# D times u as a diagonal TensorE product that opens the state-sum bank, in a fused attention, Mamba and FFN kernel

## The reference, cut to what matters

```python
def step(h, inp):
    dt_t, B_t, C_t, u_t = inp
    dA = jnp.exp(dt_t[..., None] * A)
    h = dA * h + (dt_t * u_t)[..., None] * B_t[:, None, :]
    y_t = jnp.einsum('ben,bn->be', h, C_t)
    return (h, y_t)
...
y = ys.transpose(1, 0, 2) + u2 * D_param
y = y * jax.nn.silu(z)
out = jnp.einsum('ble,ed->bld', y, W_out)
```

## Time and profile before

| | |
|---|---|
| median of 3 runs | 778.05 us (777.77 to 780.21) |
| the profiled execution's own time | 779.12 us |
| its span (first to last instruction) | 777.3 us |
| mean granted TensorE clock | 0.989 |
| busy: TensorE, VectorE, ScalarE, GpSimd | 713.9, 685.4, 640.2, 608.8 us |

### The profile page before, as it was taken

The page is one execution under the profiler, slowest core; times in us unless marked ns, Lnnn a source line. Parts: engine busy times, 40 slices in busy tenths (PEclk is TensorE's granted clock), DMA queues, the critical chain, the costliest instruction groups (busy, mean ns, idle before and its releaser), DMA issues. The chain is left out here.

```text
span 777.3 us, 21855 instructions
## 1 busy us (share of the span) xinstructions
PE 713.9 (92%) x8036; PEld 406.7 (52%) x8036; DVE 685.4 (88%) x1138; ACT 640.2 (82%) x1282; POOL 608.8 (78%) x598
## 2 busy tenths in 40 slices
PE   6889999998999989999999999979998999887888
PEld 4676644644565446556555356445464453352456
DVE  6987428998999999899999899999999999898983
ACT  4778687999989999998889999888979866865633
POOL 5004336888998989778898789999999999999871
PEclk9999997999999999999999999999999999999999
DMA  6000014442624152323415161525261525344410
GB/s 212 3 4 2 3 45 151 132 128 87 186 68 156 36 175 95 100 95 110 138 47 192 52 229 58 178 89 175 68 192 45 177 83 177 109 153 136 149 42 28
DMA packets 45003, 83.63 MB, mean 108 GB/s; under 512 B 5081, under 2 KB 5730, under 8 KB 44898
## 3 DMA queue, kind: packets, MB, share of 16 engines
q1 hardware_dynamic: 44898, 82.25, 33.1%
HBM read 71.22 MB, written 11.01 MB: 106 GB/s over the span
## 5 line engine op out<-in xcount | busy, mean ns | idle before, releaser
L1804 POOL TENSOR_TENSOR d<-d,cr 128x1024 f32<-128x1024 f32 x128 | 299.9, 2352 | 16.1 <-DVE d L1305 5.8
L1622 ACT ACTIVATE ps<-dt,An 128x512 f32<-128x512 f32 x252 | 172.2, 696 | 39.6 <-DVE d L1305 38.5
L1305 DVE TENSOR_TENSOR_SCAN d<-ps,hl,d 128x512 f32<-128x512 f32 x128 | 157.6, 1267 | 3.7 <-ACT ps L1622 3.2
L1305 DVE TENSOR_TENSOR_SCAN d<-ps,d 128x512 f32<-128x512 f32 x128 | 150.1, 1207 | 6.6 <-ACT ps L1622 6.2
L886 PE MATMUL ps<-h,w 128*128 128x512 f16 (+1 forms) x512 | 114.5, 376 | 8.5 <-DVE h L1237 8.2
L1293 DVE TENSOR_TENSOR d<-ps,du 128x512 f32<-128x512 f32 x173 | 112.2, 675 | 6.1 <-PE ps L975 3.8
L1790 POOL TENSOR_TENSOR d<-du,br 128x512 f32<-128x512 f32 x79 | 99.8, 1274 | 8.3 <-PE ps L975 5.4
L886 PEld LDWEIGHTS ps<-h,w 128*128 128x128 f16 x512 | 47.7, 98 | 77.8 <-DVE h L1237 20.8
L975 PE MATMUL ps<-d,cst 128*32 128x512 f32 x512 | 68.1, 604 | 2.9 <-POOL d L1804 2.9
L897 PEld LDWEIGHTS ps<-w,h 128*128 128x128 f32 x496 | 58.2, 192 | 8.3 <-issue 5.5
L824 PE MATMUL ps<-cst,sx 128*128 128x128 f32 x384 | 56.1, 283 | 6.1 <-ACT sx L1453 4.1
(11 more groups left out here) (185 smaller groups left out, 1374.7 us busy)
## 6 DMA issues: line engine op xcount, KB each, us to landing
cr<-bcd SPq DMA_DIRECT2D x64, 256.0 KB, 3.3
br<-bcd SPq DMA_DIRECT2D x64, 256.0 KB, 3.2
dt<-dtd SPq DMA_DIRECT2D x64, 256.0 KB, 3.6
du<-dud SPq DMA_DIRECT2D x64, 256.0 KB, 3.7
dtd<-sR SPq DMA_DIRECT2D x16, 256.0 KB, 2.6
dud<-sE SPq DMA_DIRECT2D x16, 256.0 KB, 2.0
X<-in_x SPq DMA_DIRECT2D x8, 256.0 KB, 6.1
out<-X SPq DMA_DIRECT2D x3, 512.0 KB, 4.6
```

Of the source, the lines that this page charges most:

```text
L1305: eng.tensor_tensor_scan(d, banks[u % NG][:, :], d, hl[:, r:r + 1] if m % 2 else 0.0, ALU.mult, ALU.add).then_inc(v_sc, 1)
L1622: eng.activation(banks[u % NG][:, :], src[:, :], ACT.Exp, scale=An[:, g:g + 1]).then_inc(s_da, 1)
L1804: eng.tensor_tensor(d, d, CR[k % NC][:, :].unsqueeze(1).to_broadcast((128, n, 512)), ALU.mult).then_inc(p_cm, n)
```

## The change

`csum_t` at w = 0 (blocks 0 to 14) first multiplies u by a 128 x 128 diagonal matrix of D_e on TensorE, into the whole bank with `start=True`; the sixteen sums of a block then add to it. VectorE's step (`gate_v`, in `yev_v`'s places) multiplies the bank by silu(z) straight into u's buffer, now waiting for `s_zs` too. GpSimd's `gate_p` goes, and all that waited for `p_gt` waits for `v_yg`. GpSimd builds the diagonals once (`dd_p`). To make room the constant `spread` goes; GpSimd builds a wider 128 x 512 form of it (`spr_p`) in the tenth D buffer before the scans begin, and the products of `bdt_t` and `bdu_t` use all 128 rows. No other place of the table changes.

```diff
-    (BLOCKS[:-1], 'gate_p yev_v'),
+    (BLOCKS[:-1], 'gate_v'),
...
+    "dd_p": [33000],
+    "spr_p": [105500],
...
+            fours = D[:, ND - 1, :]
             def bdt_t(u):
+                if u > 1:
+                    eng.wait_ge(v_dr, u - 1)
                 bank = bank_of["bdt", u] = turn((s_da, u + 1))
                 eng.wait_ge(v_md, 2)
-                q = slice(32 * u, 32 * u + 32)
-                eng.matmul(bank[:, :], spread[q, :], sR[q, :], start=True, stop=True).then_inc(t_bdt, 1)
+                if u == 0:
+                    eng.wait_ge(p_spr, 1)
+                eng.matmul(bank[:, :], fours[:, 128 * u:128 * u + 128], sR[:, :], start=True, stop=True).then_inc(t_bdt, 1)
...
                 bank = bank_of["y", m, eb]
+                whole = (m, eb) != BLOCKS[-1]
+                if w == 0 and whole:
+                    if k == 0:
+                        eng.wait_ge(p_dd, 2)
+                    eng.wait_ge(s_silu, m + 1)
+                    eng.matmul(bank[:, :], Dd[:, eb, :], u2[m % 2][:, eb, :], start=True, stop=False, skip_group_check=True)
...
                     t = eng.matmul(bank[32 * q:32 * q + 32, :], csel, D[:, (4 * k + q) % ND, :],
-                                   start=(w == 0), stop=(w == 3))
+                                   start=(w == 0 and not whole), stop=(w == 3), skip_group_check=True)
...
-                eng.wait_ge(p_gt, 2 * m + 2)
+                eng.wait_ge(v_yg, 2 * m + 2)
...
+                if u == ND - 1:
+                    eng.wait_ge(t_bdt, FIRST)
+                    eng.wait_ge(t_bdu, FIRST)
...
-            def yev_v(m, eb):
-                if m == eb == 0:
-                    eng.wait_ge(l_w2, 16)
-                yg = u2[m % 2]
+            def gate_v(m, eb):
+                eng.wait_ge(s_zs, m + 1)
                 eng.wait_ge(t_y, 8 * m + 4 * eb + 4)
-                eng.scalar_tensor_tensor(yg[:, eb, :], yg[:, eb, :], Dp[:, eb:eb + 1], bank_of["y", m, eb][:, :],
-                                         ALU.mult, ALU.add).then_inc(v_yg, 1)
+                eng.tensor_tensor(u2[m % 2][:, eb, :], bank_of["y", m, eb][:, :], zs[m % 2][:, eb, :], ALU.mult).then_inc(v_yg, 1)
...
+            def spr_p():
+                eng.wait_ge(v_set, V_END)
+                eng.wait_ge(l_w1, 16)
+                eng.tensor_scalar(D[:, ND - 1, :].rearrange("p (c s) -> p c s", s=4), ident.unsqueeze(2).to_broadcast((128, 128, 4)), 1.0, 0.0, ALU.mult, ALU.add).then_inc(p_spr, 1)
...
-            def gate_p(m, eb):
-                yg = u2[m % 2]
-                eng.wait_ge(s_zs, m + 1)
-                eng.wait_ge(v_yg, 2 * m + eb + 1)
-                eng.tensor_tensor(yg[:, eb, :], yg[:, eb, :], zs[m % 2][:, eb, :], ALU.mult).then_inc(p_gt, 1)
+            def dd_p():
+                eng.wait_ge(l_w1, 16)
+                eng.wait_ge(l_w2, 16)
+                for eb in range(2):
+                    eng.tensor_scalar(Dd[:, eb, :], ident, Dp[:, eb:eb + 1], None, ALU.mult).then_inc(p_dd, 1)
```

More of the change, by code:

```diff
@@ L23 @@
 CONST, NCONST = {}, 0
-for _name, _n in (("ident", 128), ("qmask", 4), ("csel", 32), ("one8", 1), ("rmask", 2), ("spread", 128)):
+for _name, _n in (("ident", 128), ("qmask", 4), ("csel", 32), ("one8", 1), ("rmask", 2)):
     CONST[_name] = (NCONST, _n)
@@ L167 @@
     ([(0, g) for g in range(8)], 'aqm_v'),
-    ([()], 'an_s lpre_p one_v vz_p'),
+    ([()], 'an_s dd_p lpre_p one_v spr_p vz_p'),
     (BATCH_HALVES[2:], 'aln_v'),
     ([(u,) for u in range(NCORE) if driver(u) == "v"], 'drive_v'),
-    (BLOCKS[:-1], 'gate_p yev_v'),
+    (BLOCKS[:-1], 'gate_v'),
     ([(NCORE - 1,)], 'out_v'),
@@ L382 @@
     "lmo_t": [730212, 731403],
+    "gate_v": [170724, 203947, 243372, 289687, 329072, 373421, 412775, 455280, 491228, 541367, 573401, 605514, 645916, 678023, 713280],
+    "dd_p": [33000],
     "lpre_p": [719305],
@@ L472, in const @@
             return cst[0:rows, at:at + n]
-        ident, qmask, csel, one8, rmask, spread = (const(n) for n in ("ident", "qmask", "csel", "one8", "rmask", "spread"))
+        ident, qmask, csel, one8, rmask = (const(n) for n in ("ident", "qmask", "csel", "one8", "rmask"))
         masks = sb("masks", [128, 288], BF16)
@@ L558, in hybrid_block @@
         hl = sb("hl", [128, NR])
+        Dd = sb("dd", [128, 2, 128])
         l_x = [sem(f"l_x{i}") for i in range(2 * NB)]
@@ L566, in hybrid_block @@
         l_t, l_q = ([sem(f"l_{x}{q}") for q in range(4)] for x in "tq")
-        v_set, v_clr, v_one, p_set, p_vz, s_ap = (sem(n) for n in ("v_set", "v_clr", "v_one", "p_set", "p_vz", "s_ap"))
+        v_set, v_clr, v_one, p_set, p_vz, s_ap, p_spr = (sem(n) for n in ("v_set", "v_clr", "v_one", "p_set", "p_vz", "s_ap", "p_spr"))
         v_ast, v_aag, p_ars, s_ano, p_ano, t_atr, s_aat, p_aap = (sem(n) for n in ("v_ast", "v_aag", "p_ars", "s_ano", "p_ano", "t_atr", "s_aat", "p_aap"))
@@ L580, in hybrid_block @@
         t_mx, s_mx, t_md, s_md, v_md, p_md, s_bp = (sem(n) for n in ("t_mx", "s_mx", "t_md", "s_md", "v_md", "p_md", "s_bp"))
-        s_da, v_dr, p_dr, v_sc, p_hl, p_cm, t_y, v_cm, v_yg, p_gt, p_lp, v_lg, t_mo, v_mo, t_bdt, t_bdu = (
-            sem(n) for n in ("s_da", "v_dr", "p_dr", "v_sc", "p_hl", "p_cm", "t_y", "v_cm", "v_yg", "p_gt", "p_lp", "v_lg", "t_mo", "v_mo", "t_bdt", "t_bdu"))
+        s_da, v_dr, p_dr, v_sc, p_hl, p_cm, t_y, v_cm, v_yg, p_dd, p_lp, v_lg, t_mo, v_mo, t_bdt, t_bdu = (
+            sem(n) for n in ("s_da", "v_dr", "p_dr", "v_sc", "p_hl", "p_cm", "t_y", "v_cm", "v_yg", "p_dd", "p_lp", "v_lg", "t_mo", "v_mo", "t_bdt", "t_bdu"))
         V_SEL, V_FFN, V_WK, V_END = 7, 17, 20, 20
@@ L958, in bdu_t @@
                 eng.wait_ge(p_md, 3)
-                q = slice(32 * u, 32 * u + 32)
-                eng.matmul(bank[:, :], spread[q, :], sE[q, :], start=True, stop=True).then_inc(t_bdu, 1)
+                if u == 0:
+                    eng.wait_ge(p_spr, 1)
+                eng.matmul(bank[:, :], fours[:, 128 * u:128 * u + 128], sE[:, :], start=True, stop=True).then_inc(t_bdu, 1)
             def csum_t(k):
@@ L999, in lmo_t @@
                 bank = bank_of["lmo", h] = banks[0 if h else 3]
-                eng.wait_ge(p_gt, 2 * NM - 1)
+                eng.wait_ge(v_yg, 2 * NM - 1)
                 eng.wait_ge(p_lp, 2)
@@ L1347, in _ @@
                     "fln_v": fln_v, "flo_v": flo_v, "fl1_v": fl1_v, "fl3_v": fl3_v, "mln_v": mln_v, "dt_v": dt_v, "dr_v": dr_v,
-                    "drive_v": drive_v, "scan_v": scan_v, "yev_v": yev_v, "mout_v": mout_v}
+                    "drive_v": drive_v, "scan_v": scan_v, "gate_v": gate_v, "mout_v": mout_v}
             for name, at in plan:
@@ L1554, in mz_s @@
                 if m >= 2:
-                    eng.wait_ge(p_gt, 2 * m - 2)
+                    eng.wait_ge(v_yg, 2 * m - 2)
                 for eb in range(2):
@@ L1824, in _ @@
             mine = {"vz_p": vz_p, "lpre_p": lpre_p, "aln_p": aln_p, "aap_p": aap_p, "akp_p": akp_p, "jsub_p": jsub_p, "jsum_p": jsum_p, "jmix_p": jmix_p, "fln_p": fln_p,
-                    "mln_p": mln_p, "dt_p": dt_p, "du_p": du_p, "drive_p": drive_p, "out_p": out_p, "gate_p": gate_p}
+                    "mln_p": mln_p, "dt_p": dt_p, "spr_p": spr_p, "du_p": du_p, "drive_p": drive_p, "out_p": out_p, "dd_p": dd_p}
             for name, at in plan:
```

3 lines of the change are left out of this document (removed).

## The result

| | before | after |
|---|---|---|
| median | 778.2 us (4 runs, 777.77 to 780.21) | 785.66 us (4 runs, 782.93 to 787.16) |
| profiled execution, span | 779.1, 777.3 us | 787.16, 785.3 us |
| mean granted clock | 0.989 | 0.989 |

The ratio of after to before is 1.0067, 95% interval [1.0036, 1.0097]; the two medians by themselves are 0.96% apart, at the upper end of that interval, as four runs of each are few. The forecast was 778.0 us, between 772 and 784.

The account below looks back on a forecast made before the run. No engine bounds the whole: TensorE and ScalarE carry 240 to 480 us, VectorE bounds 480 to 717. Terms -0.5 - 0.7 + 2.5 + 0.5 - 1.5 - 0.3 = 0.0 us gave a median of 778.0 us, between 772 and 784 8 times in 10.

Parts of the forecast that it names:

- the term of the diagonal product: TensorE, fifteen block openings: 14.7 us more work, priced at 2.5 us for five openings and 0.5 us for ten.
- For the other ten ... taken as 0.5 us: Ten openings outside 240 to 480 us: 0.5 us lost, bounds 0 to 9.8, with 23.6 us TensorE free in 480 to 717.
- the openings from 240 to 480: Five openings where TensorE has 7.9 us free: 2.5 us lost, the middle of bounds 0 and 4.9.
- GpSimd's gate: 15 GpSimd instructions, 19.2 us, removed: 0.5 us won through VectorE's waits for GpSimd, bounds 0 and 4.2.
- The turn at the drive near 706: GpSimd's drive at 706.37 would wait for sums until 707.0, so the pairs behind it come 0.6 us later than now.
- VectorE's step: Fifteen block ends on VectorE, 682 instead of 726 ns each: 0.7 us won, bounds 0 and 0.7.
- The product's length: Each diagonal product on TensorE takes 0.98 us, read from a similar identity product in the trace.
- The first tiles: Before the first scans, 128-row products longer but clock kept up (6 in 10): 1.5 us won, bounds 2.9 won, 2.1 lost.
- Constants and load: Building constants on GpSimd costs nothing, `spr_p` at most 1.28 us in a 9.11 us gap; smaller load wins 0.3 us.
- The first, with 784: Five openings in 240 to 480 cost 4.9 us, first tiles lose 2.1: 784 us; 0.32 including its halves.
- The second (773): GpSimd's relief from 480 to 717 frees VectorE of 4.2 us, clock gives 2.9: 773 us; faster side 0.32.
- The signs that the forecast named for being wrong: VectorE's idle time from 142 to 740 us changing by more than 3 us, or the clock falling at new places.

Follow-up runs that it names:

- e4: Changed kernel with the diagonal product moved behind the first four sums of its block; 1.0076 [1.0053, 1.01] to the kernel before.
- e7: Changed kernel with GpSimd kept busy by a same-size product at each old gate's place; 1.0052 [1.0031, 1.0073] to the kernel before.
- e8: Changed kernel with 79 instead of 126 filler products between 609 and 715 us; 1.0055 [1.0035, 1.0076] to the kernel before.
- e2: Changed kernel without its fifteen diagonal products, u D left out; 0.9957 [0.9932, 0.9982] to the kernel before.
- e12: Changed kernel without diagonal products, GpSimd kept busy at its old gate's places, first run; 0.999 [0.9973, 1.0008] to the kernel before.
- e13: Changed kernel without its diagonal products, run again on another chip; 0.9961 [0.9939, 0.9982] to the kernel before.
- e14: Changed kernel without diagonal products, GpSimd kept busy at its old gate's places, second run; 0.9955 [0.9935, 0.9974] to the kernel before.
- e1: Kernel before with only the 128-row spread form for the first four tiles; 1.0007 [0.9985, 1.0029] to the kernel before.
- e17: Kernel before with only the 128-row first tiles, repeated on another chip; 1.0003 [0.9978, 1.0027] to the kernel before.
- e11: Kernel before without the 20 filler products from 263 to 458 us; 1.0095 [1.0062, 1.0127] to the kernel before.
- e16: Changed kernel with the new way only for stretches 6 and 7 (three openings), 128-row first tiles kept; 0.9974 [0.9952, 0.9995] to the kernel before.
- e18: Changed kernel with the new way only for stretches 6 and 7 (three openings), repeated; 0.9961 [0.9941, 0.9982] to the kernel before.

## Why the prediction was wrong

**The step that failed is the term of the diagonal product, in its second half: "For the other ten ... taken as 0.5 us".** For the openings from 240 to 480 the mechanism and the size were right; for the other ten idle time was taken for slack. With the four traces that have the product and all else of the change (after, e4, e7, e8) against the four without it (e2, e12, e13, e14), the mean span is 784.7 against 776.8 us. By the block steps these 7.9 us lie as follows:

| openings | predicted | traces |
|---|---|---|
| five, from 240 to 480 (block 2 to 7) | 2.5 | 3.0 |
| block 0's, before its step | part of 0.5 | 1.0 |
| two, blocks 1 and 2 | part of 0.5 | 1.2 |
| seven, blocks 8 to 14 | part of 0.5 | 2.5 |
| behind block 14 | 0 | 0.2 |

So the ten openings that were put at 0.5 us cost 4.7.

The five that I looked at were sized well. I priced the others by idle time in a stretch, 23.6 us of TensorE from 480 to 717, and that isn't slack: seven new products of 0.98 us, which would fit into it three times over, cost 2.5 us there. It is waiting for VectorE and ScalarE, which comes at its own moments. "Buffers are ten deep" is no cover either: e4, whose sums end as early as before, is no faster. That the attention, FFN and dt products behind the opening carry the delay is the reading that is left, not a thing tested by itself. The 1.0 us at block 0 is the least certain of the table, since the front differs by over 2 us between traces of one kind, and so do the late ones with their clock drops.

That the rest of the change won 3.2 us by the times, where the forecast had 3.0, is luck: the parts, read below, were not what the forecast had them.

Point by point:

- *GpSimd's gate*, 0.5 us: nothing at the end that the times resolve (e13, e14; e7), 0.7 to 1.4 us between blocks 12 and 13 by the traces. The turn at the drive near 706 came as written; GpSimd in the kernel after:

```profile
703.54 6.99 POOL L1824 TENSOR_TENSOR d<-d,cr 128x1024 f32<-128x1024 f32 x3
712.28 1.27 POOL L1810 TENSOR_TENSOR d<-du,br 128x512 f32<-128x512 f32 x1 [1.75 <-PE ps L988]
```

- *VectorE's step*, 0.7 us: 15 x (726 - 670) ns = 0.84 us of busy time, a little over its bound.
- *The product's length*, 0.98 us: right. TensorE at 263.63, to be read beside the earlier trace rows, and VectorE's drive behind it, whose wait of 0.26 us is now 1.12, nearly the whole product:

```profile
263.63 1.02 PE L980 MATMUL ps<-u,dd 128*128 128x512 f32 x2
264.58 1.06 PE L988 MATMUL ps<-d,cst 128*32 128x512 f32 x8
...
265.71 1.29 DVE L1310 TENSOR_TENSOR d<-ps,du 128x512 f32<-128x512 f32 x2 [1.12 <-PE ps L988]
```

- *The first tiles*, 1.5 us won: the step came as reckoned. The eight products, against the earlier trace rows, run from 120.02 to about 127.1, 2.0 us longer, and the clock, against the earlier trace rows, is 1.00 where it was 0.50 to 0.65:

```profile
120.02 1.98 PE L967 MATMUL ps<-sE,d 128*128 128x512 f32 x4
...
126.13 1.02 PE L959 MATMUL ps<-sR,d 128*128 128x512 f32 x2
```

```profile
132.00:134.00 2.00, 1.15 (x7) 0.47 (x5) 1.93 (x4) 1.75 (x4) 1.64 (x2) 1.00 0.26 93
```

  Block 0's step is 1.4 us earlier, and with the first tiles alone 3.3 and 4.0, more than the bound of 2.9. What I hadn't asked is how much of a front gain reaches the end: e1 and e17 say none that can be measured. (Where the forecast puts the sum 3 us higher should the change cure nothing, its own terms make 1.5 + 2.1 = 3.6.) And the drop is not the same in every execution: in e11, whose front is that of the kernel before, the clock over 118 to 142 is 0.93, not 0.79. In all traces with 128-row products it is 1.00, which fits the cause that I gave but is not proof of it.
- *Constants and load*: `spr_p` took 0.63 us in a gap of over 8 us. The 0.3 us of the load can't be seen in a median.
- *The two rivals.* The first, with 784, came nearest, but not by its mechanism: its five openings were to cost 4.9 us and cost 3.0, VectorE's waits for TensorE from 240 to 480 rose from 4.8 to 6.4 us and not by 5, and its other half, the drop that stays, did not happen. What made up the number were the openings outside its stretch. The second (773) had its gain from GpSimd, and GpSimd gave nothing like its 4.2 us.
- *The signs that the forecast named for being wrong* both came. VectorE's idle time from 142 to 740 was to change by no more than 3 us; it went from 31.0 to 41.4 us, before and after:

```profile
142.00:740.00 598.00, 555.46 (x5808) 302.32 (x5806) 566.96 (x845) 523.80 (x1028) 541.30 (x493) 1.00 0.39 123
```

```profile
142.00:740.00 598.00, 565.17 (x5814) 306.40 (x5813) 556.56 (x834) 519.24 (x1017) 516.22 (x474) 0.99 0.38 122
```

  And the clock falls at new places: 0.56 and 0.59 in 516 to 520, where the product runs at half pace.

```profile
515.80 0.75 PE L825 MATMUL ps<-cst,sx 128*128 128x128 f32 x4 [1.66 <-ACT sx L1467]
516.35 1.92 PE L980 MATMUL ps<-u,dd 128*128 128x512 f32 x2
518.20 1.76 PE L988 MATMUL ps<-d,cst 128*32 128x512 f32 x8
```

Open: how often the drop near 516 comes in each kernel, and what holds the clock in e16 and e18; the traces are one or two for each kernel. That the products cost more than the rest gives is settled by the ratios of after, e4, e7 and e8, all above 1 with their intervals.

## What to carry to other kernels

An engine's idle time in a stretch is not slack for new work: look at what ends each idle time and what is queued behind the new instruction. Here the first part of an addition cost little and the rest nearly its full length. Work taken from an engine that hardly anyone waits for is worth little, however busy it looks: GpSimd was 95% busy in a third of the kernel, and 19 us less of it brought nothing that the times could resolve. The same addition can pay at one place and cost at another: with three late openings the kernel was faster than before, with fifteen slower. Take fillers out only with a run beside it: 5 us less of them made this kernel 7.4 us slower.

## What the runs showed of the hardware

The same wait of TensorE may be followed by a fall of the clock or not. The first tiles alone were traced twice, with the same rows and the same idle time (1.72 and 1.73 us) at 509, and the clock fell in one (e17: 0.50 in the two microseconds behind) and not in the other (e1). First e1, then e17:

```profile
509.69 0.66 PE L824 MATMUL ps<-cst,sx 128*128 128x128 f32 x4 [1.72 <-ACT sx L1463]
510.27 1.07 PE L981 MATMUL ps<-d,cst 128*32 128x512 f32 x8
```

```profile
509.19 0.71 PE L824 MATMUL ps<-cst,sx 128*128 128x128 f32 x4 [1.73 <-ACT sx L1463]
509.83 1.94 PE L981 MATMUL ps<-d,cst 128*32 128x512 f32 x8
```

with the stretch behind it:

```profile
510.00:512.00 2.00, 2.00 (x40) 0.69 (x36) 2.00 (x5) 2.00 (x5) 2.00 (x3) 0.50 0.03 8
```

e17 has a second drop at 524 (0.79 over 520 to 528), and with both it lost 3.1 us between blocks 8 and 9. Of 20 traces 10 have one or two drops between 505 and 532 us. In front of the fillers near 710 it is the same: of nine traces with a wait of 3.47 us there two kept the clock (before, e12), of eight with 2.96 us two (e16, e18). Such drops are as large as the whole effect of some edits, so one profile of each of two kernels can't tell their ends apart; the block steps ahead of the drop can.
